# Second attention: scores computed as rows for the maximum and again transposed for the probabilities

## The reference

```
scores = einsum('bhqd,bhkd->bhqk', q, k_h) / sqrt(16)
scores = where(causal, finfo.min, scores)
attn   = softmax(scores, axis=-1)
ctx    = einsum('bhqk,bhkd->bhqd', attn, v_h)
return ctx.reshape(b, t, 512) @ Wo
```

## Time and profile before

| | |
|---|---|
| median of 3 runs | 1173.53 us |
| profiled execution, its span | 1172.01 us, 1170.4 us |
| TensorE (PE) busy, instructions | 1135.4 us (97%), 6634 |
| VectorE (DVE) | 787.2 us (67%), 2463 |
| ScalarE (ACT) | 705.8 us (60%), 1646 |
| GpSimd (POOL) | 410.8 us (35%), 342 |
| mean granted TensorE clock | 0.997 |

### The profile page before, as it was taken

How to read it: one execution, slowest core, us unless ns; L and a number is a source line. 1 busy time by engine, 2 the same in 40 slices (tenths; PEclk the granted TensorE clock), 3 DMA queues, 4 the chain that set the end, 5 groups by cost and what they waited for, 6 DMA issues and landing times. The chain is left out here.

```text
span 1170.4 us, 19511 instructions
## 1 busy us (share of the span) xinstructions
PE 1135.4 (97%) x6634; PEld 953.0 (81%) x6634; DVE 787.2 (67%) x2463; ACT 705.8 (60%) x1646; POOL 410.8 (35%) x342
## 2 busy tenths in 40 slices
PE   7999999999999999999999999999999899999997
PEld 5888888888888888888888778888888677777786
DVE  6767776766776777767677752222336899999775
ACT  6656665656765666665665644453112899999524
POOL 4654554354544445544452513334013210020200
PEclk9999999999999999999999999999999999999999
DMA  6011111111110111100100012222001223321001
GB/s 231 19 39 42 39 28 28 28 35 38 46 28 19 37 37 37 36 28 19 37 19 28 1 46 72 63 80 74 1 18 29 56 67 81 99 50 34 1 1 72
DMA packets 30346, 51.04 MB, mean 44 GB/s; under 512 B 5680, under 2 KB 6576, under 8 KB 30256
## 3 DMA queue, kind: packets, MB, share of 16 engines
q1 hardware_dynamic: 29680, 48.85, 14.7%
q10 hardware_dynamic: 576, 1.05, 0.2%
HBM read 38.35 MB, written 2.10 MB: 35 GB/s over the span
## 5 line engine op out<-in xcount | busy, mean ns | idle before, releaser
L491 POOL TENSOR_TENSOR turned<-turned,sin 128x512 f32<-128x512 f32 x73 | 94.6, 1296 | 276.3 <-ACT turned L347 276.3
L363 ACT ACTIVATE probs<-probs,neg_max 128x256 f32<-128x256 f32 (+1 forms) x256 | 119.7, 473 | 11.3 <-DVE neg_max L591 11.3
L1488 ACT ACTIVATE a_probs<-a_probs,a_neg_max 128x512 f32<-128x512 f32 (+3 forms) x256 | 122.6, 562 | 0.1
L1672 DVE CUSTOM_DVE_ANT_0 a_probs<-bank,a_mask 128x512 f32<-128x512 f32 (+3 forms) x256 | 109.8, 485 | 6.0 <-PE bank L1892 6.0
L494 POOL TENSOR_TENSOR turned<-turned,by_cos 128x512 f32<-128x512 f32 x73 | 101.2, 1386 | 11.1 <-DVE by_cos L564 5.7
L96 PE MATMUL bank<-wo_hi,oT_hi 128*128 128x512 f32 x256 | 100.3, 392 | 1.7 <-DVE oT_lo L654 1.7
L745 PE MATMUL bank<-xT_hi,wq_hi 128*128 128x512 f32 x256 | 101.4, 396 | 0.0
L745 PE MATMUL bank<-xT_lo,wq_hi 128*128 128x512 f32 x256 | 100.2, 392 | 0.0
L745 PE MATMUL bank<-xT_hi,wq_lo 128*128 128x512 f32 x256 | 100.1, 391 | 0.0
L96 PE MATMUL bank<-wo_hi,oT_lo 128*128 128x512 f32 x256 | 99.9, 390 | 0.0
L96 PE MATMUL bank<-wo_lo,oT_hi 128*128 128x512 f32 x256 | 99.7, 389 | 0.0
(11 more groups left out here) (234 smaller groups left out, 3155.4 us busy)
## 6 DMA issues: line engine op xcount, KB each, us to landing
staged<-weights SPq DMA_DIRECT2D x70, 256.0 KB, 2.7
f_staged<-weights_f SPq DMA_DIRECT2D x33, 256.0 KB, 2.7
a_q_stack<-a_qT_hi SPq DMA_DIRECT2D x64, 64.0 KB, 2.0
rows<-x_rows SPq DMA_DIRECT2D x2, 1024.0 KB, 7.2
a_k_stack<-a_kT_hi SPq DMA_DIRECT2D x64, 32.0 KB, 2.0
a_q_stack<-a_qT_lo SPq DMA_DIRECT2D x32, 64.0 KB, 2.0
out<-rows SPq DMA_DIRECT2D x8, 256.0 KB, 2.0
a_raw<-weights_qkv SPq DMA_DIRECT2D x4, 384.0 KB, 4.8
```

The source lines that it names most:

```text
L363: act.activation(probs[:, s % 2, h, 0:width], probs[:, s % 2, h, 0:width], ACT.Exp, bias=neg_max[:, s % 2, h:h + 1], scale=SCALE0, accum_o ...
L491: pool.tensor_tensor(at, at, sin[:, :], ALU.mult).then_inc(sin_done, 1)
L1488: act.activation(row_probs(s, qt), row_probs(s, qt), ACT.Exp, bias=neg_max[:, h, qt:qt + 1], scale=-1.0).then_inc(exp_done, 1)
L1672: dve.tensor_tensor_reduce(row_probs(s, qt), ps_s[bank][:, at:at + seen], mask[:, SEQ - seen:SEQ], -SCALE1, HIGHEST, ALU.add, ALU.min, neg ...
```

## The change

The loop goes over 32 pairs of heads instead of 64 heads. The probabilities are no longer computed as rows and turned; instead the scores are computed twice.

- The stacks hold each head's 48 rows in one half of the partitions (rows from 0 and from 64). There are three buffers. A stack takes 6 key DMAs and 12 query DMAs, all of 16 rows.
- The row scores of a pair go to two neighbouring PSUM banks. The causal mask is added by six bf16 matmuls with an identity. VectorE only reduces them to maxima (`find_maxima`), 8 columns for a pair.
- TensorE turns the 8 columns into 8 rows (`turn_maxima`), ScalarE copies them to SBUF (`read_maxima`), and SP copies each row of 128, by 8 DMAs, under the queries as a 49th row (`load_maxima`). The keys have -1 there.
- `key_scores` multiplies again with keys and queries exchanged: keys in the partitions, the maximum already subtracted. ScalarE takes the exponential from PSUM straight into the place that the values' product reads. GpSimd sets what lies beyond the diagonal to zero (`keep_causal`, four `affine_select` per pair).
- The evacuation of the output moves from VectorE to ScalarE. The three bank pairs are shared by both kinds of scores; scores and maxima run two pairs ahead.

The core of the diff:

```
+PAIR_DMAS = 16 * 2 * PARTS
+STACK_DMAS = 3 * PAIR_DMAS
+MAX_DMAS = 16 * 2 * SEQ_TILES
...
             def load_queries(u, pair, arrived):
                 b, g = divmod(u, KV1)
-                first = (g % 2) * GROUP_COLS + pair * PAIR_ROWS
-                for part, source in enumerate((qT_hi, qT_hi, qT_lo)):
-                    sp.dma_start(q_stack[part * PAIR_ROWS:(part + 1) * PAIR_ROWS, u % 2, pair, :].bitcast(F32),
-                                 source[first:first + PAIR_ROWS, g // 2, b * SEQ:(b + 1) * SEQ].bitcast(F32)).then_inc(arrived, 16)
+                for n, at in enumerate((0, HALF_ROWS)):
+                    first = (g % 2) * GROUP_COLS + (2 * pair + n) * HD1
+                    for part, source in enumerate((qT_hi, qT_hi, qT_lo)):
+                        to = at + part * HD1
+                        sp.dma_start(q_stack[to:to + HD1, u % BUFFERS, pair, :].bitcast(F32),
+                                     source[first:first + HD1, g // 2, b * SEQ:(b + 1) * SEQ].bitcast(F32)).then_inc(arrived, 16)
...
+            def load_maxima(p):
+                u, pair = divmod(p, 2)
+                sp.wait_ge(max_read, p + 1)
+                for n, at in enumerate((0, HALF_ROWS)):
+                    for qt in range(SEQ_TILES):
+                        row = n * SEQ_TILES + qt
+                        sp.dma_start(q_stack[at + STACK:at + STACK + 1, u % BUFFERS, pair, qt * P:(qt + 1) * P].bitcast(F32),
+                                     max_rows[row:row + 1, p % 2, :].bitcast(F32)).then_inc(max_in[p % 2], 16)
...
+            for u in range(BUFFERS):
+                load_stacks(u)
+            for p in range(PAIRS1):
+                load_maxima(p)
+                u = p // 2
+                if p % 2 == 1 and u >= 1 and u + 2 < UNITS1:
...
+                    sp.wait_ge(keys_scored, STEPS * (p - 1))
+                    load_stacks(u + 2)
...
+            def exps(p, step):
+                act.wait_ge(keys_scored, STEPS * p + step + 1)
...
+                act.activation(pair_probs(p)[:, :, at:at + width], ps_pair[KEY_BANKS[step]][:, :, 0:width], ACT.Exp,
+                               scale=SCALE1).then_inc(exp_done, 1)
...
+            def keep_causal(p, step):
+                pool.wait_ge(exp_done, STEPS * p + step + 1)
+                for kb in KEY_STEPS[step]:
+                    at = step * SEQ + TURNED_AT[kb]
+                    probs = pair_probs(p)[:, :, at:at + P]
+                    last_kept = pool.affine_select(probs, probs, [[0, 2], [1, P]], ALU.is_ge, nothing, base=0,
+                                                   channel_multiplier=-1)
+                last_kept.then_inc(kept, 1)
...
+                for qt in SCORE_STEPS[step]:
+                    at = SCORES_AT[qt]
+                    found = dve.tensor_reduce(by_tile[:, :, qt:qt + 1], ps_pair[SCORE_BANKS[step]][:, :, at:at + (qt + 1) * P],
+                                              mybir.AxisListType.X, ALU.max)
...
+            def key_scores(p, step):
...
+                    pe.wait_ge(max_in[p % 2], MAX_DMAS * (p // 2 + 1))
...
+                        part = slice(rows_at, rows_at + STACK + 1)
+                        mm = pe.matmul(banks[:, n, TURNED_AT[kb]:TURNED_AT[kb] + SEQ - kb * P],
+                                       k_stack[part, u % BUFFERS, kb * P:(kb + 1) * P],
+                                       q_stack[part, u % BUFFERS, pair, kb * P:SEQ], start=True, stop=True,
+                                       skip_group_check=True)
```

More of the change, by code:

```diff
@@ L1357, in attention1 @@
         ps_q, ps_kv, ps_part = [psum[n] for n in Q_BANKS], [psum[n] for n in KV_BANKS], [psum[n] for n in PART_BANKS]
-        ps_s, ps_t, ps_o = psum[0:3], psum[3:6], psum[6:8]
+        ps_pair = [t["psum"][:, 2 * n:2 * n + 2, :] for n in range(3)]
+        ps_o, ps_m = psum[6], psum[7]
+        keep, causal = mask[:, 0:P], mask[:, P:3 * P]
         ps_out, ps_y, ps_side = psum[0:2], psum[2:4], psum[6:8]
@@ L1508, in _ @@
                     act.wait_ge(v_done, SEQ_TILES)
[L1509 to L1521, removed]
+            copy_values(TILES - 1)
+            act.wait_ge(v_done, TILES)
+            for p in range(-1, PAIRS1):
+                if p + 1 < PAIRS1:
+                    read_maxima(p + 1)
+                if p >= 0:
+                    exps(p, 0)
+                if p >= 3 and p % 2 == 1:
+                    evacuate((p - 3) // 2)
+                if p >= 0:
+                    exps(p, 1)
+                    exps(p, 2)
+                if p in PARTS_IN_LOOP:
+                    high_part(PARTS_IN_LOOP[p])
             def high_out(tile):
@@ L1545, in scale_last @@
                                scale=last.inv_deviation[:, tile:tile + 1]).then_inc(last.normed, 1)
-            for tile in range(4):
+            high_out(0)
+            evacuate(UNITS1 - 1)
+            for tile in range(1, 4):
                 high_out(tile)
@@ L1706, in _ @@
                     low_part(j)
-            maxima(0)
-            maxima(1)
+            dve.wait_ge(pads_set, 3)
+            for step in range(STEPS):
+                find_maxima(0, step)
             rotate(TILES - 1)
[L1710 to L1720, removed]
+            for p in range(-1, PAIRS1 + 1):
+                if p + AHEAD1 < PAIRS1:
+                    find_maxima(p + AHEAD1, 0)
+                if p >= 4 and p % 2 == 0:
+                    join((p - 4) // 2)
+                if p + AHEAD1 < PAIRS1:
+                    find_maxima(p + AHEAD1, 1)
+                    find_maxima(p + AHEAD1, 2)
+                if p in PARTS_IN_LOOP:
+                    low_part(PARTS_IN_LOOP[p])
             steps = [0]
@@ L1795, in _ @@
             low_out(0)
+            low_out(1)
             join(UNITS1 - 1)
-            for tile in range(1, 4):
+            for tile in range(2, 4):
                 low_out(tile)
@@ L1916, in apply @@
+            def apply(u, step):
+                if u == 0 and step == 0:
                     pe.wait_ge(v_done, TILES)
                     pe.wait_ge(pads_set, 2)
[L1918 to L1919 removed]
                     pe.wait_ge(part_lo, len(TURNS))
[L1921 to L1925 removed]
@@ L1954, in _ @@
                 if tile == TILES - 1:
-                    scores(1)
+                    scores(0, 1)
+                    scores(0, 2)
                     pe.wait_ge(v_done, TILES - 1)
```

355 lines of the change are left out of this document (194 added, 161 removed).

## The result

| | median | range | ratio to before, 95% interval |
|---|---|---|---|
| before | 1172.74 us (4 runs) | 1171.94 to 1173.54 | |
| after | 1349.45 us (4 runs) | 1348.36 to 1350.68 | 1.151 [1.149, 1.153] |

The change costs 177 us. The forecast was 1336, the range 1278 to 1352. The profiled execution took 1350.51 us with a span of 1348.8, 178.4 more than before's span. In the trace the first output projection begins at 1272.16 us instead of 1093.59, 178.6 later: all of the loss lies ahead of it, from the stacks to the end of the loop, and nothing behind it.

A forecast was written before the change was run, and what follows sets the result against it. SP's DMA issues at 0.634 us were taken to bound the loop: three starting stacks, 490 issues, seven loads, waits and the end shift the first projection by 162.6 us, giving 1336 us against the median; range 1278 to 1352.

The forecast's parts named there:

- first rows leave SP: Start of the second attention: SP issues three stacks, 54 DMAs at 0.634 us, from 895.2, so until 929.4 us.
- 490 issues at 0.634 and 7 loads: Loop on SP: 13 stacks of 18 and 32 pairs of 8 rows, 310.7 us, plus seven weight loads at about 0.5.
- SP's own waits: Four pairs without a stack (2, 3, 30, 31): SP waits 0.8 us each for a 4.5 us turnaround.
- SP's last issue to the first projection: Loop's end: landing 1.4 us after SP is done, key scores and exponentials 3.5, outputs' turn 3.8, last values 0.7.
- shift of the first projection: First output projection moves from 1093.59 to 1256.2 us, 162.6 later; what follows is unchanged.
- The price of a one-row DMA: SP's issue of a maxima row: between 0.43 and 0.634 us, taken as 0.634; 0.43 would give 1290 us.
- The signs: Trace: 54 issues before the first row at about 929, gapless loop, 21.6 us units, TensorE's longest waits naming the maxima's DMA.
- Cheaper rows: Rival on SP: one-row DMAs cost less; 0.43 us gives 1290. Chance 0.16 at 0.43 to 0.6, 0.04 cheaper yet still slower.
- GpSimd as the bound: Rival in the loop: selects over 2.7 us set the pace, 1350 to 1400 us; chance 0.03, shared with the clock.
- the clock as the bound: Rival in the loop: TensorE at 1.2 GHz, all its pieces on the path, 1350 to 1400 us; chance 0.03, shared with GpSimd.
- The faster case: Rival: issues run beside each other, SP is no bound and the pair goes at TensorE's pace: 1158 us; chance 0.02.
- free rows: Rows at nearly no SP cost: stacks and little-hidden pair turnarounds end SP near 1140, giving 1235 us, still slower.

The follow-up runs named there:

- the two runs that only change their number: Changed kernel with 2 row DMAs a pair instead of 8: 1263.06 us; changed kernel with 16 a pair, each row in two halves: 1506.15 us.
- the run with the clock up: Changed kernel with idle matmuls added on TensorE ahead of its two waits for DMAs, to keep its granted clock up: 1355.35 us.
- two rows on ScalarE: Changed kernel with two whole-row DMAs a pair instead of eight of a quarter, issued by ScalarE instead of SP: 1241.59 us.
- three changes of what stands where: On the changed kernel with two-head stacks (1183.91 us), successively: SP's order split, 1180.52; row DMAs on ScalarE, 1172.32; VectorE's division before its maximum search, 1162.57.
- The layout for two heads: Changed kernel with before's two-head stacks, both heads' maxima as two rows brought by one DMA a pair, 14 issues a unit: 1183.91 us.

## Why the prediction was right, and where it was off

The mechanism was right: SP's issues set the loop, and the two runs that only change their number move the time, with SP's own waits counted, by 0.64 us for each issue removed and 0.65 for each added. The number was 13 us short. The sum, term by term, on the profiled execution's clock:

| step | forecast | measured | off |
|---|---|---|---|
| first rows leave SP | 929.4 | 929.20 | -0.2 |
| 490 issues at 0.634 and 7 loads | 314.2 | 318.5 | +4.3 |
| SP's own waits | 3.2 | 9.1 | +5.9 |
| SP's last issue to the first projection | 9.4 | 15.3 | +5.9 |
| shift of the first projection | 162.6 | 178.6 | +16.0 |

- *The price of a one-row DMA.* 0.634 was taken between 0.43 and 0.634. Measured: 0.589 of issue and the same step of 0.63, though it carries 0.5 KB and not 32. The term is 4.3 us short because nine of the issues took 0.95 to 1.33 us (one of them in the two that took 1.82 instead of 1.22 at 957.25), 5.1 us more than nine usual ones. What makes these long stays open.
- *SP's own waits.* The places were right, the pairs with no stack between, at the start (24.22 us for 32 rows that need 20.3) and at the end (24.72). The size was not: two waits of 4.0 us together at the start and one of 4.7 at the end, where the sum had four of 0.8. At the end the maxima of two pairs later came 8.6 us after a pair's landing (1238.23 to 1246.84), not 4.5: the sum had left out that the values' matmuls (L2007, 3.7 us here) stand between them in TensorE's order. The half clock lengthens this, as the wait of 2.2 us in the run with the clock up suggests.
- *The end.* TensorE's half clock was left out of the sum and kept for the range as up to 12 us. It is only a part of this term. The last row landed 3.60 us after its issue, where the sum had 2.0. In the run with the clock up it landed after 1.69 us; so of the 4.7 us that its end is shorter, 1.9 are the landing and 2.8 are left for the clock, with the last values in 1.93 us instead of 3.64. Why the row landed late stays open. The chain of waits at the end of the loop (start us, us, what):

```profile
1236.53 1.70 DMA a_q_stack<-a_max_rows
...
1240.33 1.86 PE banks L2007 x8
...
1242.92 1.86 PE banks L2007 x16
...
1256.24 3.60 DMA a_q_stack<-a_max_rows
```

- *The range.* Its upper end had 12 us for the clock alone. The long issues, the waits and the late landing used them up as well, so that it held, by under 3 us, was in part luck.
- *The other engines.* VectorE's reductions were put at 3.3 us a pair: 4 x 0.822. ScalarE's exponentials at 1.02 on the mean: 0.88. GpSimd's selects were put at 0.73, the upper of two neighbours, and took 0.406, next to the lower one, so GpSimd was busy 13 to 22% of the loop and not a quarter. All were hidden, as said:

```profile
L1673 POOL TENSOR_SCALAR_AFFINE_SELECT f_pT<-f_pT 128x256 f32<-128x256 f32 x96 | 37.9, 406 | 259.6 <-ACT f_pT L1530 259.6
```

- *The signs.* All 54 issues ahead of the first row, the row at 929 and the loop without gaps came as named. TensorE's longest waits name the stacks first (62.3 us) and the maxima second (46.1); both are SP's.
- *The rivals.* Cheaper rows fell by the row price; GpSimd as the bound fell with its idle time, and the clock as the bound with the covered units of the run with the clock up, which are no shorter. The faster case needed 34 issues in 11 us. One reason given against it was misread: the trace of before does have issues under 0.4 us, loads from DRAM of 0.33, though none of those from SBUF to SBUF was under 0.5. A version faster than before came only with 14 issues a unit, 12 of them on SP, and with VectorE's division moved ahead.
- *What the forecast said of free rows*, that they would still leave 1235 us: its own steps from SP's end at 1140 give 1229. The run that comes nearest, two rows on ScalarE, took 1241.59, and its trace shows the order that was given as the reason, a stack behind a pair's maxima. But its rows are not free and the half clock is on its path, so that the numbers lie so close is not shown to be more than luck.

## What to carry to other kernels

Count the DMAs of a loop on each engine that issues them and multiply by the step in that engine's order of time (here 0.63 us from SBUF to SBUF, for 256 bytes as for 64 KB), because no busy share shows this engine. When a layout makes operands in smaller pieces, price the pieces first: the same arithmetic was 15% slower with 34 DMAs a unit and 1% slower with 14. Once the queue has air, look at what stands behind what in each engine's order; the last 21 us, to 0.8% faster than before, came from three changes of what stands where, one of which put the two row DMAs of a unit on another engine.

## What the runs showed of the hardware

- Matmuls on two halves of the partitions run beside each other. In the run with the clock at 0.97, the two heads' matmuls with 49 rows and 512 columns begin 0.003 us apart (at 1118.46), and a pair takes as long as one: eight were busy for 2.0 us together, 0.50 a pair, at 494 ns each. With 98 rows and the clock at 1.00 the second begins 0.31 us behind the first (at 1003.07), and eighteen took 6.4 us, 0.71 a pair. The layout for two heads gives this up and wins all the same.

```profile
L1995 PE MATMUL banks<-a_q_stack,a_k_stack 49*128 49x512 f32 x8 | 2.0, 494 | 2.8 <-DMA a_q_stack<-a_max_rows 2.8
```

```profile
L1987 PE MATMUL banks<-a_q_stack,a_k_stack 98*128 98x512 f32 x18 | 6.4, 434 | 0.0
```

- TensorE's clock fell to 0.57 to 0.69 in stretches of after where it was busy 28 to 36 us of 50, and was 0.84 to 0.97 where the added matmuls made that 37 to 42. Busy time alone doesn't tell the clock: with two rows on ScalarE TensorE was busy 41 to 44 us of 50 at 0.67 to 0.76. In the units that SP covers, the time did not follow the clock.
- A row that is four partitions of 128 lands as one partition of 512 by a single DMA, at the price of any other issue (0.58 us).
